# A graph-network kernel: VectorE is made to follow GpSimd's gathers, and the first gathers are issued without a copy of their indices

## The chip, the core and the metric

The kernel runs on one core of a Trainium2 chip. The metric is the device time of one execution in microseconds (us), as the median of several runs. The core has five engines with queues of their own: PE (TensorE, matmuls), DVE (VectorE), ACT (ScalarE), POOL (GpSimd) and SP (SyncE, which here only issues DMAs). They wait for each other through semaphores. A gather by a list of row indices is issued by POOL, with one instruction for each tile of 128 rows.

## What is computed

Two layers of a graph network over 3125 nodes and 53125 edges, the edges sorted by destination. Cut to what matters here, with `x` of 3125 x 256:

```python
# layer 0
messages = edge_val[:, None] * x[src]
neighbor = segment_sum(messages, dst, 3125)
side = (neighbor + neighbor * x) @ W2.T + b2
out = leaky(x @ W1.T + b1 + side)
x = layernorm(x + out / norm(out))
# layer 1
e = relu(edge_attr @ ee_w1 + ee_b1) @ ee_w2 + ee_b2
agg = segment_sum(x[src] + e, dst, 3125)
h = mlp((1 + eps) * x + agg)          # 256 -> 1024 -> 1024 -> 256, two layernorms
x = layernorm(x + relu(layernorm(x + h)))
```

## The kernel before

**Stages.** The first stage does layer 0 and the part of layer 1 that doesn't need its result (the sum over edges of `relu(edge_attr @ ee_w1 + ee_b1)`). The second stage gathers rows of the table that the first one stored, sums them and runs the three dense layers. The change touches the first stage alone.

**Tiles.** Nodes lie in 25 blocks of 128, edges in tiles of 128: 17 tiles for each block and 8 for the last, 416 in all. The tiles of a block are handled as pairs (`PAIRS`, line 41): eight pairs of two and a ninth (k = 8) of one.

**One pair (q, k) of the first stage.**
- POOL gathers the rows `x[src]` of each of its tiles into `raw[:, j]` (line 777; line 757 in the first block). Before each even j it waits for `message` of the same pair one block earlier, which freed that part of `raw`.
- ACT (`highs`, line 1408) scales each gathered tile into the high half of `msg` (line 1414), then takes relu of the edge network's result out of PSUM (line 1417).
- DVE makes the low halves: `low_neighbour` (line 1800) reads `raw` and `msg`, both in SBUF, once for each tile; `low_edge` (line 1806) reads PSUM and `msg` and counts up `message`.
- DVE also writes the one-hot matrices `oh` that say which row of the block each edge goes to (`near_oh`, line 1781, through `equal`, line 134: one tensor_scalar of 128x128 for each tile).
- PE multiplies `oh` by `msg` and adds up in PSUM (lines 932 and 934), and runs the edge network (line 927) three pairs ahead, into a ring of three banks.

**Order on DVE.** It is written out by hand in `near_block` (line 1873). In step s of block b, DVE first writes one-hots (needed three sums later), then waits for `high` of the pair three on (`LEAD = 3`) and does its `low_neighbour` and `low_edge`; pieces of the tails of the two blocks before (`tail`, line 1819: normalisation, table rows) are put in between, and `take_s` after step 1.

**Start.** SP issues `dst` (line 515), then `src` (line 516), then the rest. POOL writes two iotas (`lane`, `base`), a memset of one row of ones in `attr` (line 739, 1x2176), waits for `src`, copies the first block's indices into three small tiles (line 746) and gathers from these. DVE meanwhile checks in how many blocks the sorted edges stray (lines 1727 to 1752), which yields `level`; every engine waits for that and then takes the path for sorted edges ("near").

**End of the stage.** After its last gather POOL prepares one-hots of source rows (line 859), and then issues eight early gathers of the second stage (line 869), once the table rows of all blocks but the last two are stored; these rows come from DVE's `tail` of block 22 (line 1858), which stands behind the last messages in DVE's order.

Of the kernel before, what the change touches and what calls it, by code (L numbers as in the profile page):

```python
# [31 lines left out]
N, E, D, ED, H = 3125, 53125, 256, 64, 1024  # L32
P = 128
BLOCKS = -(-N // P)
TILES = E // N
LAST_ROWS = N - (BLOCKS - 1) * P
LAST_TILES = -(-E // P) - (BLOCKS - 1) * TILES
# [3 lines left out]
PAIRS = [(0, 2), (2, 2), (4, 2), (6, 2), (8, 2), (10, 2), (12, 2), (14, 2), (16, 1)]  # L41
NP = len(PAIRS)
# [2 lines left out]
ZERO_ROW = ROWS_PADDED  # L45
assert LAST_TILES % 2 == 0
LEAD = 3
ENDING = 3
CHUNKS = [(0, 6), (6, 6), (12, 5)]
KD = D // 128  # L50
# [7 lines left out]
def wait(eng, sem, value):  # L58

    if isinstance(value, int) and value <= 0:  # L60
        return
    eng.wait_ge(sem, value)
# [80 lines left out]
def has_pair(b, k):  # L143

    return exists(b) and (k < LAST_PAIRS or not is_last(b))
# [44 lines left out]
def gnn_program(nc, x, xT, src, dst, weight, attrT, w1T, w2T, bias01, bias02, eps_in, ee_w1, ee_b1row, ee_b1,  # L190
# [6 lines left out]
    with ExitStack() as keep:  # L197
# [14 lines left out]
        src_all = sb("src_all", [P, BLOCKS * TILES], I32)  # L212
# [16 lines left out]
        with ExitStack() as ca:  # L229
# [3 lines left out]
            def ma(name):  # L233
                return sem(name)
# [8 lines left out]
            attr = sa("attr", [ED + 1, TILES * P], F32)  # L243
            raw_base = nc.sbuf_base
            raw = sa("raw", [P, TILES, D], F32)
# [52 lines left out]
            src_in, weight_in, we1_in = ma("src_in"), ma("weight_in"), ma("we1_in")  # L298
            idx_ready = [ma(f"idx_ready{c}") for c in range(3)]
            attr_in = [ma(f"attr_in{c}") for c in range(3)]  # L300
            gathered = [ma(f"gathered{j}") for j in range(TILES)]
            xs_in, xr_in, xT_in = ma("xs_in"), ma("xr_in"), ma("xT_in")

            pool_ready = ma("pool_ready")
            prep = ma("prep")
            bad_ready, bad_total, level_ready = ma("bad_ready"), ma("bad_total"), ma("level_ready")
            rel_ready = ma("rel_ready")
# [3 lines left out]
            message = ma("message")  # L311
# [9 lines left out]
            da = ma("da")  # L321
            dd_end = [ma(f"dd_end{n}") for n in range(ENDING)]
            da_end = [ma(f"da_end{n}") for n in range(ENDING)]
# [184 lines left out]
        def _(sp):  # L508
            def load_attr(n, c):
# [2 lines left out]
                sp.dma_start(attr[0:ED, j * P:(j + m) * P],  # L512
                             attrT[:, bass.ds((n * TILES + j) * P, m * P)]).then_inc(attr_in[c], 16)

            sp.dma_start(dst_i[:, :, :].rearrange("p b j -> p (b j)"), dst).then_inc(edges_in, 16)
            sp.dma_start(src_all[:, :], src).then_inc(src_in, 16)
            sp.dma_start(w_sb[:, :], weight).then_inc(weight_in, 16)
            sp.dma_start(we1[0:ED, :], ee_w1).then_inc(we1_in, 16)
            sp.dma_start(we1[ED:ED + 1, :], ee_b1row).then_inc(we1_in, 16)
# [141 lines left out]
            with sp.If(lvl > 0):  # L661
# [11 lines left out]
                for b in range(1, BLOCKS - 1):  # L673
# [9 lines left out]
                    if 3 <= b < 3 + len(weights):  # L683
                        load, k = weights[b - 3]
# [47 lines left out]
        def _(pool):  # L732
# [2 lines left out]

            pool.iota(base[:, :], [[P, BLOCKS], [0, TILES]], base=0, channel_multiplier=0,
                      allow_small_or_imprecise_dtypes=True).then_inc(pool_ready, 1)
            pool.wait_ge(pool_ready, 2)
            pool.memset(attr[ED:ED + 1, :], 1.0).then_inc(pool_ready, 1)
            pool.wait_ge(pool_ready, 3)  # L740
            pool.wait_ge(src_in, 16)

            def stage_idx(n, c):

                j0, m = CHUNKS[c]
                pool.tensor_copy(idx[c][:, :], src_all[:, tile_cols(n, j0, m)]).then_inc(idx_ready[c], 1)

            def gather_chunk(q, c, start=0):
                j0, m = CHUNKS[c]
                pool.wait_ge(idx_ready[c], q + 1 + (1 if start else 0))  # L750
                pool.nop(nofuse=True)
                for j in range(j0, j0 + m):
                    if j % 2 == 0:

                        wait(pool, message, start + NP * (q - 1) + j // 2 + 1)
                        pool.nop(nofuse=True)
                    pool.indirect_dma_start(
                        out=raw[:, j, :], out_offset=None, in_=x,
                        in_offset=bass.IndirectOffsetOnAxis(ap=idx[c][:, j - j0:j - j0 + 1], axis=0),
                    ).then_inc(gathered[j], 16)  # L760


            for c in range(3):
                stage_idx(0, c)
            for c in range(3):
                gather_chunk(0, c)
            pool.wait_ge(level_ready, 1)
            lvl = pool.value_load(level[0:1, 0:1])

            def near_gathers(q):  # L770

                for j in range(LAST_TILES if is_last(q) else TILES):
                    if j % 2 == 0:

                        pool.wait_ge(message, NP * (q - 1) + j // 2 + 1)
                        pool.nop(nofuse=True)
                    pool.indirect_dma_start(  # L777
                        out=raw[:, j, :], out_offset=None, in_=x,
                        in_offset=bass.IndirectOffsetOnAxis(
                            ap=src_all[:, q * TILES + j:q * TILES + j + 1], axis=0),  # L780
                    ).then_inc(gathered[j], 16)

            def near_program(path):
# [4 lines left out]
            def general_program():  # L788
                for j in range(TILES):
                    pool.wait_ge(gathered[j], 16)  # L790

                def general_block(b):
                    with pool.Fori(0, BLOCKS) as n:
                        q = b * BLOCKS + n
                        for c in range(3):

                            pool.wait_ge(message, NP * q + 3 * c + 3)
                            stage_idx(n, c)
                            gather_chunk(q, c, NP)

                general_block(0)
                with pool.Fori(1, BLOCKS) as b:
                    general_block(b)
                second_general()
# [105 lines left out]
        @block.tensor  # L910
        def _(pe):

            pe.wait_ge(pool_ready, 3)
            pe.wait_ge(bad_ready, 1)
            pe.matmul(ps_d[0:1, 0:len(EDGES)], ones_c[:, :], bad_sum[:, :], start=True, stop=True)\
              .then_inc(bad_total, 1)
# [76 lines left out]
            def near_block(path, b, bank):  # L993

                for s in range(NP):
                    q, k = (b, s + LEAD) if s + LEAD < NP else (b + 1, s + LEAD - NP)
                    if has_pair(q, k):
# [13 lines left out]
            def near_program(path):  # L1011
                for k in range(LEAD):
                    edge_layer(0, k)
# [3 lines left out]
                near_block(path, before, 1)  # L1017
                edge_layer(last, LEAD)
                near_step(path, last, 0, 0)
# [376 lines left out]
        def _(act):  # L1396
# [50 lines left out]
            def near_block(path, b, par):  # L1447
                for s in range(NP):
                    q, k = (b, s + LEAD) if s + LEAD < NP else (b + 1, s + LEAD - NP)
                    if has_pair(q, k) and not (is_last(q) and k >= LEAD - 1):  # L1450
                        highs(path, q, q, k)
# [11 lines left out]
            def near_program(path):  # L1463
                for k in range(LEAD):
                    highs(path, 0, 0, k)
# [254 lines left out]
        @block.vector  # L1720
        def _(dve):

            dve.memset(ones_c[:, :], 1.0).then_inc(prep, 1)
            dve.memset(ln_eps[:, :], LN_EPS).then_inc(prep, 1)
            dve.memset(zero_oh[:, :], 0.0).then_inc(prep, 1)
# [24 lines left out]
            dve.tensor_scalar(holds[:, :], ps_d[0:1, 0:len(EDGES)], 0.0, None, ALU.is_equal).then_inc(prep, 1)  # L1750
            dve.wait_ge(prep, n_prep + 1)
            dve.tensor_tensor(level[:, :], holds[:, 0:1], holds[:, 1:2], ALU.add).then_inc(level_ready, 1)
            dve.wait_ge(pool_ready, 3)
            dve.wait_ge(level_ready, 1)
            dve.wait_ge(weight_in, 16)
            lvl = dve.value_load(level[0:1, 0:1])
# [62 lines left out]
            def tail(b, n, par, lag=1):  # L1819
# [40 lines left out]
                else:  # L1860
# [9 lines left out]
            TAIL_2 = {(1, 1): 2, (1, 2): 3, (2, 0): 4, (3, 1): 5, (3, 2): 6, (4, 1): 7, (4, 2): 8, (4, 3): 9,  # L1870
                      (6, 0): 10, (7, 1): 11}

            def near_block(path, b, bank, places=range(NP)):
                def fill(s, place):
                    if exists(b - 1) and (s, place) in TAIL_1:
                        tail(b - 1, TAIL_1[s, place], 1 - bank)
                    if exists(b - 2) and (s, place) in TAIL_2:
                        tail(b - 2, TAIL_2[s, place], bank)

                for s in places:  # L1880
                    q, k = (b, s + LEAD) if s + LEAD < NP else (b + 1, s + LEAD - NP)
                    j0, m = PAIRS[k]
                    if s <= 5:
                        near_oh(path, b, s + 3)
                    if s == 5:
                        near_oh(path, b, SUMS - 1)
                    if s >= 6 and exists(b + 1):
                        if s == 6:
                            near_oh(path, b + 1, 0)
                        if s <= 7:  # L1890
                            near_oh(path, b + 1, 1, s - 6)
                        else:
                            near_oh(path, b + 1, 2)
                    if has_pair(q, k):
                        dve.wait_ge(high, NP * q + k + 1)
                        for j in range(j0, j0 + m):
                            low_neighbour(q, j)
                    fill(s, 0)
                    if has_pair(q, k):
                        low_edge(k)  # L1900
                    for place in range(1, 4):
                        fill(s, place)
                    if s == 1 and exists(b - 1):
                        take_s(b - 1, SUMS * b, 1 - bank)
# [454 lines left out]
```

## Time and profile before

| | |
|---|---|
| median of 3 runs | 1189.99 us (1189.46 to 1193.68) |
| the profiled execution | 1194.22 us |
| its span, first to last instruction | 1192.4 us |
| first stage, up to POOL's last gather of it | 552.1 us |
| busy over the span | PE 93%, PE weight load 78%, DVE 80%, ACT 53%, POOL 71% |

How to read it: "busy" counts an instruction from its start to its end, so that one that stands blocked inside its own duration counts as busy too. An idle time is put down to what ended it: a DMA that landed, an instruction of another engine, or "issue", in which the engine waited for nothing that the profile shows. In a timeline a line "x2" is two like instructions merged into one, with their common time. For POOL's gathers, the duration is the time on the engine, and the landing of the data comes later.

### The profile page before, as it was taken

The numbers are of one execution on the slowest core, as the hardware profiler recorded it, in microseconds if no ns is written. First come the engines' busy times: TensorE is split into PE (matmuls) and PEld (weight loads), VectorE is DVE, ScalarE is ACT, GpSimd is POOL, SyncE is SP. The second block draws the span as 40 slices with busy tenths as digits, with TensorE's granted clock in tenths as the row PEclk, the third lists the DMA queues.
The fourth block names the chain that finished last, engine by engine and source line by source line (L and its number), as shares of the span: only waits on it lengthen the run. The fifth ranks groups of instructions, "written<-read, shape, count | busy, mean of one in ns | idle before, by whom it ended". The sixth has DMA issues, their size and how long they took to land.

```text
span 1192.4 us, 21565 instructions
## 1 busy us (share of the span) xinstructions
PE 1110.5 (93%) x5734; PEld 931.3 (78%) x5734; DVE 949.5 (80%) x2765; ACT 633.3 (53%) x1526; POOL 843.8 (71%) x859
## 2 busy tenths in 40 slices
PE   6899899899999999898689999999999999999996
PEld 4777677777777777677478888888888888888885
DVE  6889889888988988989657777777777777777765
ACT  4566556556656665665625445534544553455453
POOL 7777777777777777778767767776777777677700
PEclk9899999998999999999799999999999999999999
DMA  7456676676666565565867777777777677777710
GB/s 198 139 159 187 170 201 194 173 209 184 179 188 182 166 175 168 161 172 155 266 179 220 216 213 200 206 211 207 207 208 213 202 206 211 209 206 202 213 64 12
DMA packets 100813, 221.45 MB, mean 186 GB/s; under 512 B 19335, under 2 KB 50945, under 8 KB 100738
## 3 DMA queue, kind: packets, MB, share of 16 engines
q0 software_dynamic: 53408, 164.16, 49.0%
q1 hardware_dynamic: 47330, 56.46, 15.5%
q8 instruction: 27, 0.44, 0.2%
q14 instruction: 48, 0.39, 0.1%
HBM read 203.71 MB, written 16.83 MB: 185 GB/s over the span
## 4 chain that ended last, share of the span: by engine, by line
PE 49%; DVE 14%; DMA 12%; POOL 11%; issue 9%; ACT 4%; POOLq 0%; DVEq 0%; ACTq 0%; SPq 0%
PE ps_z L1155 28%; DMA raw<-in_x,src_all 11%; POOL raw L777 10%; PE ps_s L1138 9%; PE ps_y L1155 6%; DVE msg L1800 5%; PE ps_tr L1222 4%; DVE msg L1806 4%; DVE oh L134 2%; ACT msg L1414 2%; ACT msg L1417 2%; DMA grow<-table_dram,early_idx 1%; POOL grow L869 1%; PE ps_z L1190 1%; PE ps_tr L1149 0%
## 5 line engine op out<-in xcount | busy, mean ns | idle before, releaser
L831 POOL DMA_INDIRECT grow<-table_dram,src_all x410 | 401.8, 980 | 162.4 <-issue 103.1
L777 POOL DMA_INDIRECT raw<-in_x,src_all x399 | 403.3, 1011 | 121.6 <-issue 107.9
L1414 ACT ACTIVATE msg<-raw,w_sb 128x256 fp32r<-128x256 f32 x416 | 198.8, 502 | 145.6 <-DMA raw<-in_x,src_all 127.9
L1155 PE MATMUL ps_z<-w_high,a 128*128 128x512 f32 x784 | 252.3, 393 | 0.5 <-DVE a L2077 0.5
L932 PE MATMUL ps_sum<-msg,oh 128*128 128x512 f32 x464 | 229.6, 495 | 16.8 <-DVE msg L1806 16.3
L927 PE MATMUL ps_e<-we,attr 65*128 65x256 f32 x832 | 226.3, 393 | 9.3 <-DVE msg L1806 7.1
L1800 DVE SCALAR_TENSOR_TENSOR msg<-raw,w_sb,msg 128x256 fp32r<-128x256 f32 x416 | 183.7, 481 | 62.8 <-ACT msg L1417 61.6
L134 DVE TENSOR_SCALAR oh<-lane,rel 128x128 fp32r<-128x128 f32 x919 | 207.6, 300 | 0.1
L927 PEld LDWEIGHTS ps_e<-we,attr 65*128 65x128 f32 x832 | 157.2, 195 | 45.9 <-issue 21.5
L934 PE MATMUL ps_sum<-msg,oh 128*128 128x512 f32 x464 | 185.3, 399 | 0.0
L1155 PEld LDWEIGHTS ps_z<-w_high,a 128*128 128x128 f32 x784 | 147.3, 188 | 30.4 <-issue 0.9
L1556 ACT ACTIVATE aF<-ps_tr,be,g 128x128 f32<-128x128 f32 x392 | 142.4, 469 | 30.6 <-PE ps_tr L1222 30.6
L1155 PE MATMUL ps_z<-w_low,a 128*128 128x512 f32 x392 | 153.0, 390 | 0.0
L1806 DVE SCALAR_TENSOR_TENSOR msg<-ps_e,msg 128x512 fp32r<-128x512 f32 (+1 forms) x220 | 144.0, 655 | 0.0
L1417 ACT ACTIVATE msg<-ps_e 128x512 fp32r<-128x512 f32 (+1 forms) x220 | 122.6, 557 | 8.2 <-PE ps_e L927 7.7
L1138 PE MATMUL ps_s<-grow,oh 128*128 128x256 f32 x910 | 122.5, 285 | 0.2 <-DMA grow<-table_dram,src_all 0.2
L932 PEld LDWEIGHTS ps_sum<-msg,oh 128*128 128x128 f32 x464 | 89.4, 193 | 42.5 <-issue 24.6
L1138 PEld LDWEIGHTS ps_s<-grow,oh 128*128 128x128 f32 x910 | 117.0, 191 | 4.2 <-issue 0.4
L2034 DVE BATCH_NORM_STATS2 bs<-ps_z 128x6 f32<-128x512 f32 x100 | 69.5, 696 | 63.1 <-PE ps_z L1155 62.9
L1562 ACT ACTIVATE fm<-fm,ln_eps 128x1 f32<-128x1 f32 x50 | 14.7, 295 | 165.6 <-DVE fm L2039 165.6
L934 PEld LDWEIGHTS ps_sum<-msg,oh 128*128 128x128 f32 x464 | 90.0, 194 | 16.2
L1155 PEld LDWEIGHTS ps_z<-w_low,a 128*128 128x128 f32 x392 | 73.8, 188 | 13.7
(147 smaller groups left out, 1442.3 us busy)
## 6 DMA issues: line engine op xcount, KB each, us to landing
attr<-in_attrT SPq DMA_DIRECT2D x50, 192.0 KB, 4.2
grow<-table_dram,src_all POOLq DMA_INDIRECT x410, 3.7
table_dram<-table SPq DMA_DIRECT2D x25, 256.0 KB
raw<-in_x,src_all POOLq DMA_INDIRECT x399, 3.2
w_raw<-in_m_w SPq DMA_DIRECT2D x12, 512.0 KB, 6.0
attr<-in_attrT SPq DMA_DIRECT2D x24, 160.0 KB, 3.3
xs<-in_x SPq DMA_DIRECT2D x25, 128.0 KB, 2.4
xTb<-in_xT SPq DMA_DIRECT2D x25, 128.0 KB, 2.7
```

The source lines that it names most:

```text
L134: ins = dve.tensor_scalar(out_[:, i, :], lanes, which[:, i:i + 1], None, ALU.is_equal)
L777: pool.indirect_dma_start(out=raw[:, j, :], out_offset=None, in_=x, in_offset=bass.IndirectOffsetOnAxis(ap=src_all[:, q * TILES + j:q * TI ...
L831: pool.indirect_dma_start(out=grow[:, j, :].bitcast(F32), out_offset=None, in_=table_dram, in_offset=bass.IndirectOffsetOnAxis(ap=src_all[ ...
L927: mm = pe.matmul(ps_e[k % 3][:, (j - j0) * D:(j - j0 + 1) * D], attr[:, j * P:(j + 1) * P], we1[:, :], start=True, stop=True)
L932: pe.matmul(ps_sum[bank][:, :], oh[:, slot, :], msg[:, j, 0, :], start=start, stop=False, skip_group_check=True)
L934: return pe.matmul(ps_sum[bank][:, :], oh[:, slot, :], msg[:, j, 1, :], start=False, stop=stop, skip_group_check=True)
L1138: mm = pe.matmul(ps_s[:, 0:D], oh[:, path.slot[c] + j - j0, :], grow[:, j, part * D:(part + 1) * D], start=c == first and j == j0 and part ...
L1155: mm = pe.matmul(acc, left[a], right[b], start=False, stop=stop and a == 1, skip_group_check=True)
L1414: act.activation(msg[:, j, 0, 0:D], raw[:, j, :], ACT.Copy, scale=w_sb[:, tile_cols(n, j)])
L1417: act.activation(msg[:, j0:j0 + m, 0, D:2 * D], ps_e[k % 3][:, 0:m * D].rearrange("p (j d) -> p j d", d=D), ACT.Relu).then_inc(high, 1)
L1800: dve.scalar_tensor_tensor(msg[:, j, 1, 0:D], raw[:, j, :], w_sb[:, tile_cols(n, j)], msg[:, j, 0, 0:D].bitcast(F32), ALU.mult, ALU.subtract)
L1806: dve.scalar_tensor_tensor(msg[:, j0:j0 + m, 1, D:2 * D], ps_e[k % 3][:, 0:m * D].rearrange("p (j d) -> p j d", d=D), 0.0, msg[:, j0:j0 + ...
```

## The change

Three edits.

1. Each gather of the first stage also counts up a new semaphore, `issued`, when the instruction on POOL has ended (`engine_sem=issued`; `gathered` still counts the landing). In `near_block`, DVE waits, before the one-hots of a step, until the gather four tiles beyond the pair of that step has ended (`follow`, `AHEAD = 4`). Where that would be past the last tile, no wait is issued.
2. The first block's gathers take their indices directly from `src_all`; the three copies are gone from the path for sorted edges. SP issues `src` ahead of `dst`.
3. The row of ones in `attr` is written by DVE as its first instruction, no longer by POOL, with a semaphore of its own (`ones_row`) that PE waits for.

```diff
+AHEAD = 4
@@ sync
+            sp.dma_start(src_all[:, :], src).then_inc(src_in, 16)
             sp.dma_start(dst_i[:, :, :].rearrange("p b j -> p (b j)"), dst).then_inc(edges_in, 16)
-            sp.dma_start(src_all[:, :], src).then_inc(src_in, 16)
@@ gpsimd
-            pool.wait_ge(pool_ready, 2)
-            pool.memset(attr[ED:ED + 1, :], 1.0).then_inc(pool_ready, 1)
-            pool.wait_ge(pool_ready, 3)
             pool.wait_ge(src_in, 16)
...
-            for c in range(3):
-                stage_idx(0, c)
-            for c in range(3):
-                gather_chunk(0, c)
+            for j in range(TILES):
+                pool.indirect_dma_start(
+                    out=raw[:, j, :], out_offset=None, in_=x,
+                    in_offset=bass.IndirectOffsetOnAxis(ap=src_all[:, j:j + 1], axis=0),
+                    engine_sem=issued,
+                ).then_inc(gathered[j], 16)
...
                             ap=src_all[:, q * TILES + j:q * TILES + j + 1], axis=0),
+                        engine_sem=issued,
                     ).then_inc(gathered[j], 16)
@@ tensor
-            pe.wait_ge(pool_ready, 3)
+            pe.wait_ge(ones_row, 1)
@@ vector
+            dve.memset(attr[ED:ED + 1, :], 1.0).then_inc(ones_row, 1)
...
-            dve.wait_ge(pool_ready, 3)
...
+            def follow(q, k):
+
+                tiles = TILES * q + PAIRS[k][0] + PAIRS[k][1] + AHEAD
+                if not isinstance(q, int) or tiles <= TILES * (BLOCKS - 1) + LAST_TILES:
+                    dve.wait_ge(issued, tiles)
+
             def near_block(path, b, bank, places=range(NP)):
...
                     j0, m = PAIRS[k]
+                    if has_pair(q, k):
+                        follow(q, k)
                     if s <= 5:
                         near_oh(path, b, s + 3)
```

## Rows read from the trace of the kernel before

**Rows 1.** The page, costliest groups: busy, mean ns | idle before, releaser.
```profile
L777 POOL DMA_INDIRECT raw<-in_x,src_all x399 | 403.3, 1011 | 121.6 <-issue 107.9
L1414 ACT ACTIVATE msg<-raw,w_sb 128x256 fp32r<-128x256 f32 x416 | 198.8, 502 | 145.6 <-DMA raw<-in_x,src_all 127.9
```
**Rows 2.** Line 777 alone, whole span: duration ns min/median/max, then issue to landing.
```profile
L777 POOL DMA_INDIRECT raw<-in_x,src_all x399: 942/948/1874, 27.6 to 551.2; - x200
...
DMA to landing us min/median/max: 2.7/3.2/6.6
```
**Rows 3.** Waits, 100 to 500 us: us in total, times, longest.
```profile
POOL raw L777 <- issue: 80.4, 264, 0.3
...
POOL raw L777 <- DVE msg L1806: 12.2, 40, 0.3
```
**Rows 4.** Windows: PE, PEld, DVE, ACT, POOL busy, clock, DMA share, GB/s.
```profile
350.00:400.00 50.00, 47.21 (x210) 37.40 (x209) 45.59 (x134) 31.42 (x77) 38.24 (x39) 1.00 0.65 183
```
**Rows 5.** Timeline of POOL: the start, and the last gather.
```profile
2.16 1.90 POOL L739 MEMSET attr<- 1x2176 f32 x1
4.13 0.86 POOL L746 COPY idx<-src_all 128x6 int32<-128x6 int32 x3
5.26 1.18 POOL L757 DMA_INDIRECT raw<-in_x,idx  x1 [0.27 <-issue]
6.74 1.27 POOL L757 DMA_INDIRECT raw<-in_x,idx  x1 [0.30 <-issue]
...
551.16 0.95 POOL L777 DMA_INDIRECT raw<-in_x,src_all  x1 [0.30 <-issue]
```
**Rows 6.** Timeline, DVE and POOL, around 118 us: a lengthened gather.
```profile
118.21 0.45 DVE L134 TENSOR_SCALAR oh<-lane,rel 128x128 fp32r<-128x128 f32 x2
118.58 0.87 DVE L1800 SCALAR_TENSOR_TENSOR msg<-raw,w_sb,msg 128x256 fp32r<-128x256 f32 x2
...
118.66 1.21 POOL L777 DMA_INDIRECT raw<-in_x,src_all  x1 [0.30 <-issue]
```
**Rows 7.** The same, around 176 us: one-hots that begin as a gather ends.
```profile
175.60 0.48 DVE L134 TENSOR_SCALAR oh<-lane,rel 128x128 fp32r<-128x128 f32 x2
175.99 0.88 DVE L1800 SCALAR_TENSOR_TENSOR msg<-raw,w_sb,msg 128x256 fp32r<-128x256 f32 x2
...
174.55 1.02 POOL L777 DMA_INDIRECT raw<-in_x,src_all  x1 [0.30 <-issue]
175.88 1.02 POOL L777 DMA_INDIRECT raw<-in_x,src_all  x1 [0.30 <-issue]
177.20 0.94 POOL L777 DMA_INDIRECT raw<-in_x,src_all  x1 [0.30 <-issue]
```
**Rows 8.** The same, around 262 us: the longest kind of gather.
```profile
262.17 0.48 DVE L134 TENSOR_SCALAR oh<-lane,rel 128x128 fp32r<-128x128 f32 x2
262.56 0.88 DVE L1800 SCALAR_TENSOR_TENSOR msg<-raw,w_sb,msg 128x256 fp32r<-128x256 f32 x2
...
262.38 1.87 POOL L777 DMA_INDIRECT raw<-in_x,src_all  x1 [0.31 <-issue]
```
**Rows 9.** Timeline, end of the first stage: POOL, then DVE.
```profile
548.44 1.16 POOL L777 DMA_INDIRECT raw<-in_x,src_all  x1 [0.30 <-issue]
...
547.57 0.69 DVE L134 TENSOR_SCALAR oh<-lane,rel 128x128 fp32r<-128x128 f32 x3
...
550.03 0.47 DVE L134 TENSOR_SCALAR oh<-lane,rel 128x128 fp32r<-128x128 f32 x2
...
558.67 0.88 DVE L1800 SCALAR_TENSOR_TENSOR msg<-raw,w_sb,msg 128x256 fp32r<-128x256 f32 x2 [0.15 <-ACT msg L1417]
```
**Rows 10.** The chain that ended last, 540 to 610 us: start, us, what.
```profile
560.15 0.34 DVE table L1858
...
560.55 2.04 DMA table_dram<-table
...
563.40 1.05 POOL grow L869
...
572.54 7.30 DMA grow<-table_dram,early_idx
```
**Rows 11.** Timeline of DVE and SP, the start.
```profile
0.74 0.40 SPq L515 DMA_DIRECT2D dst_i<-in_dst  x1
...
0.89 0.17 DVE L1725 MEMSET zero_oh<- 128x128 f32 x1
3.23 1.07 DVE L1727 CAST dst_f<-dst_i 128x425 f32<-128x425 int32 x1 [2.18 <-DMA dst_i<-in_dst]
...
10.04 0.48 DVE L1907 MEMSET s_r<- 128x512 f32 x1 [0.91 <-DVE level L1752]
```

More of the change, by code:

```diff
@@ L301, in gnn_program @@
             gathered = [ma(f"gathered{j}") for j in range(TILES)]
+            issued = ma("issued")
             xs_in, xr_in, xT_in = ma("xs_in"), ma("xr_in"), ma("xT_in")
             pool_ready = ma("pool_ready")
+            ones_row = ma("ones_row")
             prep = ma("prep")
@@ L746, in stage_idx, with gather_chunk @@
                 pool.tensor_copy(idx[c][:, :], src_all[:, tile_cols(n, j0, m)]).then_inc(idx_ready[c], 1)
-            def gather_chunk(q, c, start=0):
+            def gather_chunk(q, c):
                 j0, m = CHUNKS[c]
-                pool.wait_ge(idx_ready[c], q + 1 + (1 if start else 0))
+                pool.wait_ge(idx_ready[c], q + 1)
                 pool.nop(nofuse=True)
@@ L753, in gather_chunk @@
                     if j % 2 == 0:
-                        wait(pool, message, start + NP * (q - 1) + j // 2 + 1)
+                        pool.wait_ge(message, NP * q + j // 2 + 1)
                         pool.nop(nofuse=True)
@@ L798, in general_block @@
                             stage_idx(n, c)
-                            gather_chunk(q, c, NP)
+                            gather_chunk(q, c)
                 general_block(0)
```

## The prediction

> **What bounds the kernel now.** I read the costliest groups first, then the waits and the timeline of the first stage, and last the chain that ended last. PE is busy 93% of the span, but busy time doesn't show what sets the pace of the first stage. ACT stands idle 127.9 us before line 1414 because a gather hasn't landed [rows 1]. The gathers come from POOL, and POOL never waits for anybody: between 100 and 500 us every idle time before line 777 is 0.3 us at most, also where DVE is named as releaser [rows 3]. From its first gather at 5.26 us to the end of the last at 552.11 us POOL issues 416 gathers with only that gap between them [rows 5]. So the first stage lasts as long as POOL's queue: 416 x (duration + 0.30 us). The duration has a floor: minimum 942 ns, median 948 ns; the mean is 1011 ns [rows 1, 2]. The 63 ns between mean and median, times 399, are 25.1 us, and this is the only time that the order of DVE's work can win from POOL.
>
> **What lengthens a gather.** I laid each of the 416 gathers beside DVE's instructions. A gather at 118.66 took 1.21 us while a `low_neighbour` (two inputs in SBUF) that began 0.08 us before it was under way [rows 6]. Its counterparts that begin 0.35 to 0.1 us ahead of a gather lengthen it by 0.04 to 0.26 us, those that begin 0.35 to 0.6 us into it by nothing; `low_edge`, which reads PSUM, at the gather's start lengthens nothing. So the phase of DVE against POOL matters, and edit 1 sets the phase.
>
> **Edit 1: does the wait bind?** I took, for each step with such a wait, the time at which DVE began its one-hots and the end of the gather that it must now see. In 164 of 215 steps DVE began earlier, by 1.6 us on average and 3.2 at most. The last two are 547.57 against a gather that ended at 549.60, and 550.03 against 552.11 [rows 9]. So the wait binds in some three of four steps. What is queued behind it on DVE: one-hots, `low_neighbour`, `low_edge`, the tail pieces and `take_s`. Who waits for these: PE's sums and its edge network, ACT's `norm`, `deviation` and `table_high`, SP's stores, and POOL through `message`. POOL asks for the message of the same pair one block back, some seven pairs, or 18 us, behind where a bound DVE stands: a delay of 3.2 us doesn't reach it. DVE doesn't fall behind for good either: it is busy 45.59 of 50 us in the fullest window [rows 4], and the start-to-start times of its instructions add up to 19.8 us for a block that takes POOL 17 x 1.315 = 22.4 us. Only after step 4, which holds 2.8 us of work ahead of a step that is due one gather later, it is late by 1.5 us, and catches up in the next. So the wait costs POOL nothing by itself, and the DVE work keeps pace.
>
> **What the phase is worth.** A bound step begins its one-hots just after a gather has ended. The nearest rows are those where this happened anyway: the one-hots at 175.60 follow a gather that ended at 175.57; the next gather took 1.02 us, the one after it 0.94 [rows 7]. There are 38 such places (one-hots 0.20 to 0.29 us ahead of a gather). In 35 of them the two gathers are together 0.09 us over 0.95; in three the first took 1.87 us [rows 8], and with these the average is 0.16. All gathers of the stage together are 0.126 us over for every two. The saving is then 0.126 - 0.088 = 0.038 us for every two gathers, 208 x 0.76 x 0.038 = 6.0 us. I take this value because the three long ones stood behind an uninterrupted row of DVE work, where a bound step has an idle DVE ahead of it. Bounds: all of the excess gone, 25.1 us; or 0.16 in place of 0.126, which costs 208 x 0.034 = 7.1 us. The semaphore that each gather now counts up on POOL isn't shown by any row. From below: it is free, as the gap of 0.30 us may hold it; from above, one DVE instruction's wait for its neighbour, about 0.03 us, on 416 gathers, 12.5 us. I take 0, since the gap is the same 0.3 whether a wait for DVE stands in it or not [rows 3], so it has room for more than issuing.
>
> The Trainium skill bears on this (page "SBUF — State Buffer", section "Who interferes with whom"): a DVE tensor_scalar in a two-port mode and any GpSimd instruction lock each other out, while a DVE instruction with two SBUF inputs disturbs only GpSimd instructions that read SBUF; the page infers that writing descriptors isn't disturbed by them. By that, only the one-hots would hurt, and moving them into the 0.30 us gap would win the whole excess. The rows speak against it in part: the lengthened gathers go with `low_neighbour` [rows 6]. It is rival A.
>
> **Edits 2 and 3: the start.** Gone from POOL ahead of the first gather are the memset (1.90 us) and the copies (0.86 us) [rows 5]. What is late next is `src`: the first load was issued at 0.74 us, and the work that waited for it began at 3.23 [rows 11]; `src` now has that place, so the first gather begins at about 3.4 in place of 5.26: 1.9 us. More of the gathers now lie beside DVE's checks; the first two, which did already, took 1.18 and 1.27 us [rows 5], so I take off 0.1 and keep 1.8 us; 1.3 if all five that now lie there are like that. `dst` comes 0.45 us later and `level` with it; POOL needs it only after 17 gathers. The memset on DVE: 128 elements took 0.17 us and 512 took 0.48 [rows 11], so 2176 take about 1.8 us, from 0.8 to 2.7, ahead of the arrival of `dst` at about 3.7; without this cover it would cost its 1.8 us on `level`, and even then nothing on POOL.
>
> **The end of the stage.** Here the wait costs. After the last gather the chain runs through DVE: the last messages, the table rows at 560.15, their store, and only then POOL's early gathers at 563.40 [rows 10]. Between the last two waits and the table rows DVE has hardly a gap; the only idle ahead of line 1800 is 0.15 us [rows 9]. DVE now begins these two steps 2.0 and 2.1 us later as seen from POOL's last gather. Of that 0.1 is covered: +2.0 us. It falls due once. What comes after (early gathers, second stage, where no instruction is changed) shifts as a whole.
>
> **The sum**, against the profiled execution of 1194.2 us: -6.0 (phase), -1.8 (start), +2.0 (end) = -5.8, so 1188.4. The profiled execution lies 4.2 us above the median of the runs; against the median it is 1190.0 - 5.8 = 1184.2 us.
>
> **Rivals.** **A, the whole excess goes:** -25.1 - 1.8 + 2.0 = -24.9, 1165 us; half of it, 1177. For it speaks that a bound DVE is idle in the gather's last part; against it that `low_neighbour` still follows the one-hots by 0.39 us, into the next gather's start, and that 0.07 was lost in just that place [rows 7]. **B, the phase is a bad one:** if the one-hots begin 0.08 us after the gather's end in place of 0.03, `low_neighbour` lies as in rows 8. Of 21 such places three lost 0.92 us, and the average of the two gathers was 0.21 over: 208 x (0.21 - 0.126) = +17.5 us, 1207 us. It decides from the point at which a pair of gathers costs over 0.126. The phase in a bound step hangs on how fast a semaphore of POOL reaches DVE, which no row shows. **C, nothing comes of it:** DVE's tail pieces shift the steps after the wait so that phases are as mixed as before; start and end cancel: 1190 us. It also covers a wait that is passed before it binds. **D, the semaphore lengthens each gap on POOL:** 0.03 x 416 = 12.5 us more than the forecast, 1197 us.
>
> **How the numbers follow.** Chances: forecast 0.42, A in whole or half 0.17, B 0.11, C 0.20, D 0.10. What is within 0.5% (6 us, about what a measurement of this kernel can tell from no change) is 1184 to 1196. The forecast lies at that edge: half of its chance counts as faster, half as the same. With A and a little of C: faster 0.42. With C and some of D: same 0.40; slower 0.18. The range leaves out the full A and the full B: 1172 to 1199.
>
> **What would show it.** Right: mean of line 777 near 0.99 us with gaps of 0.30, first gather near 3.4 us, one-hots 0.03 to 0.1 us behind a gather's end in most steps, more DVE idle put down to line 777, and POOL's early gathers 13 us behind its last gather of the stage in place of 11.3. Wrong: a gap above 0.30, a mean above 1011 ns, more gathers over 1.8 us, POOL waiting for line 1806, or a second stage of another length.

## The result and the profile after

The changed kernel takes 1177.74 us (median of 4 runs, 1176.62 to 1179.83) against 1189.72 us (1188.5 to 1193.68) of the kernel before on the same chip: ratio 0.9896, 95% interval 0.9869 to 0.9923, some 12 us or 1.0% less. The forecast was 1184.2 us in a range of 1172 to 1199: the time lies in it, on the side forecast, and the gain is twice the 5.8 us of the sum. The ratios and intervals here and below are taken over the fast executions alone of a kernel that also has a slower state, and so needn't be the quotient of the medians beside them. Between the two profiled executions the spans differ by 14.4 us (1192.4 to 1178.0); the one of before lay 4.2 us above its median, that of after 2.1.

The costliest groups of the page after (busy, mean ns | idle before, releaser), to be read beside [rows 1]:

```profile
L778 POOL DMA_INDIRECT raw<-in_x,src_all x399 | 389.5, 976 | 121.6 <-issue 108.5
...
L135 DVE TENSOR_SCALAR oh<-lane,rel 128x128 fp32r<-128x128 f32 x919 | 212.0, 301 | 24.3 <-DMA raw<-in_x,src_all 24.0
L1416 ACT ACTIVATE msg<-raw,w_sb 128x256 fp32r<-128x256 f32 x416 | 194.4, 501 | 69.7 <-DMA raw<-in_x,src_all 60.4
L1802 DVE SCALAR_TENSOR_TENSOR msg<-raw,w_sb,msg 128x256 fp32r<-128x256 f32 x416 | 182.8, 477 | 15.9 <-ACT msg L1419 14.3
```

Three things stand in these rows. The mean gather fell from 1011 to 976 ns, and the idle time before it is 121.6 us as before: the semaphore on POOL costs nothing. The one-hots, which never waited, now wait 24 us; the profile puts this down to the gather's DMA, but it is the new wait for the end of the instruction on POOL. ACT's idle ahead of line 1416 halved, but none of it was saved: up to 560 us ACT is idle 219 us in place of 222, and what is gone ahead of this line now stands ahead of others of ACT's lines, which wait for the later DVE. The long gathers are gone: the longest takes 1.29 us, against 1.87 in [rows 2].

Line 778 alone over the whole span (duration ns min/median/max):

```profile
L778 POOL DMA_INDIRECT raw<-in_x,src_all x399: 942/946/1292, 25.3 to 535.0; - x200
```

The start, the last gather and the first early gather in POOL's timeline, beside [rows 5] and [rows 10]:

```profile
1.25 0.84 POOL L739 IOTA base<- 128x425 f32 x1
3.63 1.10 POOL L763 DMA_INDIRECT raw<-in_x,src_all  x1 [1.53 <-DMA src_all<-in_src]
5.04 0.95 POOL L763 DMA_INDIRECT raw<-in_x,src_all  x1 [0.31 <-issue]
...
535.03 1.03 POOL L778 DMA_INDIRECT raw<-in_x,src_all  x1 [0.30 <-issue]
...
549.48 1.05 POOL L871 DMA_INDIRECT grow<-table_dram,early_idx  x1 [3.08 <-DMA table_dram<-table]
```

This splits the 14.4 us of the two spans. The first gather begins at 3.63 in place of 5.26: -1.6. From there to the end of the last gather it is 532.4 us in place of 546.9: -14.4. From the last gather to the first early gather 13.4 us in place of 11.3: +2.1. The rest of the span is 628.5 in place of 629.0: -0.5.

**A bound step**, that is one in which DVE comes to the new wait before the gather has ended and is held. Timeline of POOL after, around 302 us:

```profile
301.47 0.95 POOL L778 DMA_INDIRECT raw<-in_x,src_all  x1 [0.30 <-issue]
302.72 0.95 POOL L778 DMA_INDIRECT raw<-in_x,src_all  x1 [0.30 <-issue]
303.97 0.95 POOL L778 DMA_INDIRECT raw<-in_x,src_all  x1 [0.30 <-issue]
```

and of DVE in the same stretch:

```profile
302.45 0.53 DVE L135 TENSOR_SCALAR oh<-lane,rel 128x128 fp32r<-128x128 f32 x2 [0.25 <-DMA raw<-in_x,src_all]
302.90 0.87 DVE L1802 SCALAR_TENSOR_TENSOR msg<-raw,w_sb,msg 128x256 fp32r<-128x256 f32 x2
303.69 0.68 DVE L1808 SCALAR_TENSOR_TENSOR msg<-ps_e,msg 128x512 fp32r<-128x512 f32 x1
```

The one-hots begin 0.03 us after the gather's end at 302.42, and `low_neighbour` 0.18 us into the next gather. I laid all steps beside the gathers as for the prediction: in 110 of 207 the one-hots begin within 0.12 us of the end of the gather that they wait for, and there both gathers that follow take 0.947 us on average: none is lengthened. (Of each of the two one-hots the line shows only the common time: the first begins at 302.45, 0.27 us ahead of the next gather, the second 0.07 us ahead of it.) In the other 97 steps the two together are 0.12 us over 0.95, as all steps were before. 110 x 0.13 us is the 14 us. What all gathers take over 0.95 us, those below it counted as nothing, is 12.2 us (26.1 before); this is called the excess from here on.

**Where it remains.** Steps 5 and 6 of a block (the ninth pair and the one after it) begin about 1.7 and 0.2 us late, behind step 4 with its 2.8 us of work, and step 2, behind `take_s`, 0.34 us late; these three are late in nearly every block, steps 3, 4 and 7 in about half of them. POOL and DVE there:

```profile
293.59 1.18 POOL L778 DMA_INDIRECT raw<-in_x,src_all  x1 [0.30 <-issue]
295.07 1.03 POOL L778 DMA_INDIRECT raw<-in_x,src_all  x1 [0.30 <-issue]
296.40 1.01 POOL L778 DMA_INDIRECT raw<-in_x,src_all  x1 [0.30 <-issue]
```

```profile
293.52 0.43 DVE L1857 TENSOR_TENSOR tb<-x,eb 128x256 f32<-128x256 f32 x1
293.86 0.48 DVE L135 TENSOR_SCALAR oh<-lane,rel 128x128 fp32r<-128x128 f32 x2
...
295.71 0.88 DVE L1802 SCALAR_TENSOR_TENSOR msg<-raw,w_sb,msg 128x256 fp32r<-128x256 f32 x2
296.51 0.42 DVE L1860 TENSOR_TENSOR table<-tb,table 128x256 fp32r<-128x256 f32 x1
```

At the start of the gather of 1.18 us a tail piece with two inputs in SBUF is under way (line 1857, begun 0.07 us before it), like `low_neighbour` in [rows 6]. Put down to the DVE instruction that was begun last before the gather, `low_neighbour` has 6.5 us of what is left, the tail pieces 4.5 and the one-hots 1.1.

### The profile page after: what moved, and what is told of

Read it like the earlier page. It is cut to its first block, busy times and chain, and to the rows that moved or that the text cites. A ratio compares the mean times of both kernels' runs of the same rounds, so it can differ in the third digit from the quotient of the medians.

```text
span 1178.0 us, 21743 instructions
## 1 busy us (share of the span) xinstructions
PE 1109.2 (94%) x5734; PEld 925.7 (79%) x5734; DVE 960.2 (82%) x2766; ACT 627.8 (53%) x1526; POOL 826.8 (70%) x855
## 4 chain that ended last, share of the span: by engine, by line
PE 53%; DVE 15%; POOL 10%; issue 9%; DMA 9%; ACT 3%; SPq 1%; DVEq 0%; POOLq 0%; ACTq 0%
PE ps_z L1157 29%; POOL raw L778 10%; PE ps_s L1140 9%; DMA raw<-in_x,src_all 7%; PE ps_y L1157 6%; DVE msg L1802 5%; PE ps_tr L1224 4%; DVE msg L1808 4%; DVE oh L135 2%; PE ps_e L929 2%; ACT msg L1416 1%; ACT msg L1419 1%; PE ps_sum L934 1%; PE ps_sum L936 1%; DVE x L1854 1%
## 5 line engine op out<-in xcount | busy, mean ns | idle before, releaser
L778 POOL DMA_INDIRECT raw<-in_x,src_all x399 | 389.5, 976 | 121.6 <-issue 108.5
L135 DVE TENSOR_SCALAR oh<-lane,rel 128x128 fp32r<-128x128 f32 x919 | 212.0, 301 | 24.3 <-DMA raw<-in_x,src_all 24.0
L1416 ACT ACTIVATE msg<-raw,w_sb 128x256 fp32r<-128x256 f32 x416 | 194.4, 501 | 69.7 <-DMA raw<-in_x,src_all 60.4
L929 PEld LDWEIGHTS ps_e<-we,attr 65*128 65x128 f32 x832 | 154.4, 194 | 51.7 <-issue 27.5
L1419 ACT ACTIVATE msg<-ps_e 128x512 fp32r<-128x512 f32 (+1 forms) x220 | 122.6, 557 | 12.0 <-PE ps_e L929 11.8
L1564 ACT ACTIVATE fm<-fm,ln_eps 128x1 f32<-128x1 f32 x50 | 14.8, 295 | 166.6 <-DVE fm L2049 166.6
```

Of the source, the lines that this page charges most:

```text
L135: ins = dve.tensor_scalar(out_[:, i, :], lanes, which[:, i:i + 1], None, ALU.is_equal)
L778: pool.indirect_dma_start(out=raw[:, j, :], out_offset=None, in_=x, in_offset=bass.IndirectOffsetOnAxis(ap=src_all[:, q * TILES + j:q * TI ...
L929: mm = pe.matmul(ps_e[k % 3][:, (j - j0) * D:(j - j0 + 1) * D], attr[:, j * P:(j + 1) * P], we1[:, :], start=True, stop=True)
L1416: act.activation(msg[:, j, 0, 0:D], raw[:, j, :], ACT.Copy, scale=w_sb[:, tile_cols(n, j)])
```

## The experiments

The theory under test: what lengthens a gather is a DVE instruction with two SBUF inputs at a certain phase of the gather, and the wait helps because it fixes that phase (**phase**). Rivals: the one-hots, a tensor_scalar, block POOL and are moved into POOL's gap (**one-hots**); DVE being later helps, whatever the phase (**delay**); the start gives more than it shows.

Runs that stand in one table shared a chip and the runs of the kernel before.

**1. No wait.** The changed kernel without edit 1's wait:

```diff
-                    if has_pair(q, k):
-                        follow(q, k)
```

> The changed kernel without DVE's wait (follow is not called); the semaphore on the gathers, the direct indices, the load order and the moved memset stay. Both theories of edit 1 expect the mean of the gathers to come back to about 1.01 us (excess over 0.95 about 25 us) and a total of 1.6 us (start) below the kernel before, some 1188 us, the end of the stage giving back nothing as DVE isn't held. If the start had a larger share in the gain than the 1.6 us that the first gather shows (3.63 against 5.26), the time would be well below 1188.

**2. The wait alone.** The kernel before, with the semaphore on its gathers and `follow` as in the change, and nothing of edits 2 and 3.

> The kernel before with edit 1 alone (semaphore and wait; POOL's memset, the index copies and the load order as before). If the wait makes the gain: mean of the gathers about 0.977 us, about 1.6 us above the changed kernel, some 1179.5 us. If the edits need each other: near 1188.

**3. The wait behind the one-hots.**

```diff
-                    if has_pair(q, k):
-                        follow(q, k)
                     if s <= 5:
                         near_oh(path, b, s + 3)
...
                     if has_pair(q, k):
+                        follow(q, k)
                         dve.wait_ge(high, NP * q + k + 1)
```

> The changed kernel with the wait moved behind the one-hots of the step, ahead of the wait for ACT. The one-hots then lie anywhere, and low_neighbour begins about 0.03 us after a gather's end, 0.27 before the next, where it lengthened that by 0.07 to 0.13 us in the kernel before. Theory 'phase of low_neighbour' (two SBUF inputs): excess of the two gathers of a bound step about 0.1 us, total 1184 to 1192. Theory 'one-hots out of the way' (tensor_scalar blocks POOL, low_neighbour doesn't): the one-hots are no longer in the gap and the excess is back as well, but the lengthened gathers are those with one-hots under way, not those with low_neighbour at their start. A third, 'any alignment does': time as the changed kernel, 1178.

**4. The last block free.**

```diff
-                    if has_pair(q, k):
+                    if has_pair(q, k) and not is_last(q):
                         follow(q, k)
```

> The changed kernel without the wait for the pairs of the last block. If holding DVE at the end costs what the traces show (13.4 us from the last gather to the first early gather against 11.3), this gives back up to 2.1 us: first early gather 11.3 to 11.8 us behind, total 1175.7 to 1176.5. If something else sets that distance: no change, 1178.

Measured (kernel before: 1191.44 us):

| | us | ratio, 95% interval | mean gather, ns | excess, us | last gather to first early gather, us |
|---|---|---|---|---|---|
| 1 no wait | 1189.56 | 0.9990 (0.9976 to 1.0004) | 1005 | 23.4 | 11.3 |
| 2 wait alone | 1179.00 | 0.9897 (0.9871 to 0.9924) | 971 | 10.6 | 13.4 |
| 3 wait behind the one-hots | 1188.34 | 0.9980 (0.9963 to 0.9997) | 999 | 21.0 | 13.2 |
| 4 last block free | 1176.46 | 0.9882 (0.9853 to 0.9911) | 971 | 10.2 | 13.4 |

Runs 1 and 2 come out as the theory has it: the wait alone makes the gain (1.0%), and the start brings 1.9 us of median, which this measurement can't tell from nothing. Run 3 holds `low_neighbour` at the same gathers, yet nearly all of the gain is gone; so it isn't the delay, nor any alignment. In 102 of its 207 steps `low_neighbour` begins 0.03 us behind a gather's end, and there the next gather is 0.083 us over 0.95 and the one after it 0. One of them, POOL and DVE of run 3:

```profile
299.61 1.09 POOL L778 DMA_INDIRECT raw<-in_x,src_all  x1 [0.30 <-issue]
301.00 1.02 POOL L778 DMA_INDIRECT raw<-in_x,src_all  x1 [0.30 <-DVE msg L1808]
302.33 0.94 POOL L778 DMA_INDIRECT raw<-in_x,src_all  x1 [0.30 <-issue]
303.57 1.03 POOL L778 DMA_INDIRECT raw<-in_x,src_all  x1 [0.30 <-issue]
```

```profile
300.74 0.47 DVE L135 TENSOR_SCALAR oh<-lane,rel 128x128 fp32r<-128x128 f32 x2
301.12 0.88 DVE L1802 SCALAR_TENSOR_TENSOR msg<-raw,w_sb,msg 128x256 fp32r<-128x256 f32 x2
...
303.31 0.87 DVE L1802 SCALAR_TENSOR_TENSOR msg<-raw,w_sb,msg 128x256 fp32r<-128x256 f32 x2
```

`low_neighbour` at 303.31 begins 0.26 us ahead of the gather of 1.03 us; at 301.12 it begins 0.12 us into a gather, and that took 1.02 us, as in [rows 7]. In the bound step of the changed kernel it is 0.18 us into the gather, and that costs nothing. What does the harm at 301.00 is not `low_neighbour`, though, but the one-hot that is under way there: see run 5.

Run 4 missed its expectation in the distance, which stayed at 13.4 us. Its two waits don't hold DVE: the last `low_neighbour` of the last of these steps begins 0.8 us behind the last gather's end with them and without. The waits up to there have already made DVE late, and the steps that follow hold as much work as POOL's last gathers leave time. Its time lies in the range expected, but for another reason: not at the end, but in its gathers, of which 133 steps are like the bound one above, in place of 110 in the changed kernel, with the same waits. The 1.3 us between the medians of two sets of runs can't be told from nothing.

**5. The second SBUF input taken away**, on the kernel before, without any wait for gathers:

```diff
-                dve.scalar_tensor_tensor(msg[:, j, 1, 0:D], raw[:, j, :], w_sb[:, tile_cols(n, j)],
+                dve.scalar_tensor_tensor(msg[:, j, 1, 0:D], ps_e[j // 2 % 3][:, 0:D], w_sb[:, tile_cols(n, j)],
```

> The kernel before (no wait, old start), with low_neighbour reading its first input from PSUM (a bank of the edge network) in place of raw; the low halves of the messages are then not what they should be, everything else is computed as before. One-hots, tail pieces and all waits stay. If it is the second SBUF input of low_neighbour that lengthens gathers: the excess over 0.95 us, 26 us in the kernel before, falls to the share of the tail pieces with two SBUF inputs, 2 to 8 us, the mean to 0.955 to 0.97 us, and the total to 1167 to 1173 us, with no wait for the gathers at all. If the one-hots (tensor_scalar) do it: excess and time stay, 1190.

> The same kernel as e5_psum_input, since on the chip of that run the kernel before itself took 1575 us and POOL didn't set the pace, so that its total says nothing. The low halves of the messages are again not what they should be. Expected where the kernel before takes about 1190 us: mean of the gathers 0.955 to 0.965 us (its excess of 26 us down to some 4.5, as on that chip), total 1167 to 1172 us if low_neighbour's second SBUF input is what lengthens gathers; 1190 if the one-hots do.

**6. AHEAD = 5.**

> The changed kernel with AHEAD = 5: each step one gather later. Theory 'phase': phases as with 4, ACT is always ready, mean 0.970 to 0.977 us; the end of the stage 1.25 us longer (first early gather 14.7 us behind the last gather): 1177.5 to 1179.5 us. Theory 'the delay helps': mean below 0.965, total below 1176. If DVE's slack doesn't do for it, POOL shows waits for messages and the time is above 1185.

> As e9_ahead5, where POOL sets the pace: phases as with 4, mean of the gathers 0.970 to 0.977 us, first early gather 14.7 us behind the last gather of the stage, 1177.5 to 1179.5 us. If it is the delay that helps and not the phase: mean below 0.965, below 1176 us.

Measured on the chip on which the kernel before takes 1189.55 us:

| | us | ratio, 95% interval | mean gather, ns | excess, us | last gather to first early gather, us |
|---|---|---|---|---|---|
| 5 input from PSUM | 1173.15 | 0.9862 (0.9841 to 0.9883) | 962 | 6.7 | 11.8 |
| 6 AHEAD = 5 | 1176.18 | 0.9892 (0.9871 to 0.9913) | 965 | 7.7 | 14.8 |

Run 5 computes the low halves from the wrong input, with as many instructions as before; `low_neighbour` takes 478 ns (481 before). Line 777 of this run:

```profile
L777 POOL DMA_INDIRECT raw<-in_x,src_all x399: 942/946/1202, 27.1 to 531.2; - x200
```

The excess falls from 26.1 to 6.7 us, so that most of it was the second SBUF input of `low_neighbour`. The total is 1 us above what was expected. But the one-hots aren't innocent, as the rest of this run shows. A gather with one-hots at its start and no instruction with two SBUF inputs near it:

```profile
264.24 0.68 DVE L1806 SCALAR_TENSOR_TENSOR msg<-ps_e,msg 128x512 fp32r<-128x512 f32 x1
264.84 0.47 DVE L134 TENSOR_SCALAR oh<-lane,rel 128x128 fp32r<-128x128 f32 x2
264.92 1.02 POOL L777 DMA_INDIRECT raw<-in_x,src_all  x1 [0.30 <-issue]
265.23 0.87 DVE L1800 SCALAR_TENSOR_TENSOR msg<-ps_e,w_sb,msg 128x256 fp32r<-128x256 f32 x2
```

In this run 56 gathers are lengthened by 0.02 to 0.12 us with a one-hot as the last instruction begun before them, 3.3 us in all, nearly all where that one-hot began 0.07 to 0.13 us ahead; the tail pieces with two SBUF inputs make 3.1 us. In the kernel before, `low_neighbour` has 17.8 us in 116 gathers and the one-hots 5.9 us in 40, of which the three long gathers are 2.8. So both the phase theory and rival A's reading hold in part: the larger part is `low_neighbour`, the smaller the one-hots.

Run 6 keeps the phase and moves every bound step by one gather. Its one-hots begin 0.03 us behind a gather's end in 134 of 211 steps, more than the 110 of the changed kernel; but runs 2 and 4 have 127 and 133 with AHEAD = 4, so that this isn't the doing of AHEAD alone. The tail piece `tb` of step 4 still meets a gather's start, in 21 gathers with 3.0 us in all; what is smaller is `low_neighbour`'s part, 2.7 us in place of 6.5. A bound step costs as little as with 4. Here from its timelines of POOL and DVE:

```profile
299.83 0.94 POOL L778 DMA_INDIRECT raw<-in_x,src_all  x1 [0.30 <-issue]
301.08 0.95 POOL L778 DMA_INDIRECT raw<-in_x,src_all  x1 [0.30 <-issue]
302.33 0.95 POOL L778 DMA_INDIRECT raw<-in_x,src_all  x1 [0.30 <-issue]
```

```profile
300.81 0.53 DVE L135 TENSOR_SCALAR oh<-lane,rel 128x128 fp32r<-128x128 f32 x2 [0.25 <-DMA raw<-in_x,src_all]
301.26 0.87 DVE L1802 SCALAR_TENSOR_TENSOR msg<-raw,w_sb,msg 128x256 fp32r<-128x256 f32 x2
```

The time was expected at 1177.5 to 1179.5 and is 1176.2, since the mean came out at 965 ns, below the expected 970. That is at the edge of what **delay** was to give (below 965 ns and 1176 us), so the total doesn't decide between the two; the bound steps and run 3 do. The end is 1.35 us longer, for a wait 1.25 us later. Against the changed kernel (ratios 0.9892 and 0.9896) no difference can be told.

**7. Runs on two chips on which another thing sets the pace.** Five kernels ran, one of them twice, where the kernel before itself takes 1575 and 1577 us. Three of these were not run elsewhere:

> The changed kernel with AHEAD = 3: DVE may start each step one gather (1.25 us) earlier. Theory 'phase': a bound step still begins 0.03 us behind a gather's end, so its two gathers cost 0; but more steps then find ACT not ready and low_neighbour begins at any time: bound and clean steps 60 to 100 in place of 110, mean 0.98 to 0.995 us, end of the stage up to 1.2 us shorter: 1179 to 1185 us. Theory 'it is the delay that helps, not the phase': excess in proportion to the delay, half way back, 1184 and above, also in bound steps.

> The same kernel as e6_two_free (AHEAD = 4, no wait for the pairs of the last two blocks), where POOL sets the pace. If the wait's hold on DVE makes the longer end: first early gather 11.3 to 12.2 us behind the last gather of the stage in place of 13.4, mean of the gathers 0.972 to 0.977, total 1175 to 1176.5 us. If the distance stays at 13.4 us, something else makes it, and the total stays at 1177 to 1178.

> Three edits on the changed kernel: AHEAD = 5; no wait for the pairs of the last two blocks; the one-hot of the last sum step written in step 2, which has slack, in place of step 5, which is short. With 5 the gathers left over 0.95 us are the ones beside steps 6 and 7, which start 0.3 us late behind steps 4 and 5; 0.2 us less work in step 5 should bring step 6 to within 0.1 us of a gather's end. Phase theory: mean 0.955 to 0.966 us, first early gather 11.3 to 12.8 us behind the last, total 1172.5 to 1175.5 us. If the shift of step 6 puts its low_neighbour or the table row into a worse place: mean 0.967 to 0.975, 1175.5 to 1178.

The kernel with the last two blocks free ran twice; this was expected of it the first time:

> The changed kernel without the wait for the pairs of the last two blocks. Freeing the last block alone left the distance at 13.4 us, since DVE had been held up to the step before and has no gap there in which to gain it back. Freed one block earlier, DVE can gain its 1.5 us of idle per block: distance 11.3 to 12.2 us; one more block of mixed phases costs about 0.6 us. Total 1.0 to 1.5 us below that of freeing one block. If the distance stays at 13.4, it isn't the wait that makes it.

| | us | kernel before, us | ratio, 95% interval |
|---|---|---|---|
| AHEAD = 3 | 1575.77 | 1575.20 | 1.0007 (0.9967 to 1.0046) |
| AHEAD = 5 | 1574.28 | 1575.20 | 0.9988 (0.9949 to 1.0027) |
| last two blocks free | 1573.27 | 1575.20 | 1.0005 (0.9970 to 1.0039) |
| last two blocks free, again | 1574.21 | 1577.36 | 0.9970 (0.9940 to 1.0000) |
| AHEAD = 5, last two blocks free, one-hot moved | 1580.98 | 1577.36 | 0.9999 (0.9947 to 1.0050) |
| input from PSUM | 1586.83 | 1575.20 | 1.0112 (1.0052 to 1.0173) |

There POOL isn't the bound any more. Waits of the run with AHEAD = 5, from 100 to 500 us (us in total, times, longest):

```profile
ACT msg L1419 <- remote: 98.2, 21, 10.0
POOL raw L778 <- DVE msg L1808: 91.7, 37, 6.6
DVE msg L1802 <- ACT msg L1419: 72.7, 15, 7.3
POOL raw L778 <- issue: 65.8, 205, 1.6
DVE msg L1802 <- issue: 47.2, 17, 7.8
```

"Remote" is a releaser that stands in no record of the core. ACT and DVE stand for 5 to 10 us at a time for it or for nothing that the profile shows, the others follow, and POOL waits for messages, which it never did in [rows 3]. In at most one of some 215 steps of a run does DVE reach the new wait before it is fulfilled, and so neither the wait nor its variants change the time. What the price of one gather is can be read even there: the excess is 4.5 us with the input from PSUM and 26.0 with AHEAD = 3. What stops the engines on these chips isn't known from these runs, nor why the input from PSUM is 1.1% slower there. AHEAD = 3, the last two blocks free and the combination in the last row but one (the one meant to beat both kernels) have no verdict where POOL sets the pace.

## Why the prediction was right, and where it was off

**What bounds the first stage:** right. Without a wait of POOL anywhere, 416 gathers of (duration + 0.30 us) are the stage: the 14.4 us that it lost are the fall of the mean (34 ns x 416 = 14 us).

**The phase term was mis-sized:** 6.0 us forecast, 14.4 in the trace. The step that failed is the price of a bound step. I took it from 38 places where one-hots happened to begin as a gather ended (0.088 us for the two gathers), and took these for the same thing. They aren't. In the twelve places like [rows 7] the second one-hot began 0.08 us ahead of the gather and `low_neighbour` 0.11 to 0.12 us into it, as DVE came out of other work; that cost 0.07. It is the one-hot's doing, since run 5 has the same cost in the same place with `low_neighbour` reading PSUM. A bound step starts from idle: its second one-hot begins 0.067 us ahead, takes 0.05 us longer, `low_neighbour` follows at 0.18, and the cost is 0.00. Some 0.01 us of phase decide. The rows had both prices for `low_neighbour` at 0.17 to 0.19 (up to 0.175 us: seven times 0.12 us and three times 0.92; from 0.180 on: seven times nothing), which should have widened the term rather than been averaged. In the other direction, fewer steps are bound than the three in four of the prediction (110 of 207): steps 2, 5 and 6 arrive late; the prediction had it for step 5 alone.

So the mechanism came as forecast, with the harmless phase set by the wait, but its size didn't: that the time lies in the range is owed to its width, which takes in half of rival A.

**The start:** forecast -1.8, trace -1.6; the first gather came at 3.63, not 3.4. `level` didn't come later: see the last section.

**The end:** forecast +2.0, trace +2.1, and its size follows the wait (no wait 11.3 us, AHEAD = 4 13.4, AHEAD = 5 14.8). The prediction blamed the last two waits; run 4 shows that these two alone don't make it. That freeing more blocks would give it back wasn't shown.

**The semaphore:** forecast 0, and the gap is 0.30 us with and without it.

**The rivals.** A (the one-hots, from the rule of the Trainium skill, page "SBUF — State Buffer", section "Who interferes with whom", and its inference that writing descriptors isn't disturbed by a second SBUF input): run 5 speaks against the inference for these gathers, since the second SBUF input of `low_neighbour` carries some three quarters of the excess. The rule on tensor_scalar agrees in part: the one-hots lengthen gathers as well, by 3.3 us in run 5, but only when begun just ahead of one; that they run in a two-port mode no run here shows. Still, the size that it gave for half of the excess (1177 us) is what came. B (a bad phase) is what run 3 made by hand: 1188 us. C and D didn't occur where POOL sets the pace; C is what happened on the two slower chips.

## What to carry to other kernels

Where GpSimd's gathers set the pace, sum up what their durations exceed the median by: here this was what the order on VectorE cost, and no engine's idle time shows it. A wait for the end of a gather, put where it makes VectorE's instructions fall into a harmless phase, cost only 2 us once, at the end of the stage, as VectorE had slack. An input in PSUM won more, without a wait, in a run that read the wrong data; what it costs to bring the right data there wasn't measured. A phase taken from look-alike places must match to some 0.01 us, or be tried.

## What the hardware showed that was not expected

**What a gather loses.** Take the DVE instruction that was begun last before a gather. If it is a one-hot, a `low_neighbour` from SBUF or a tail piece with two full SBUF inputs (`tb`, `y`, `table`), still under way, and begun more than 0.07 us ahead, the gather takes longer by the time from its own start to the start of DVE's next instruction, less 0.043 us. With anything else it takes its 0.946 us. This gives 96% of the 3304 durations of the eight traces in which POOL sets the pace to within 0.012 us. An example is the gather at 118.66 in [rows 6]: the next `low_neighbour` begins 0.313 us into it, so it should lose 0.270, and takes 1.208 us, 0.262 more than 0.946. If the instruction begins later, the gather mostly loses nothing and the instruction does: the second one-hot of a bound step takes 0.326 us in place of 0.28. So it looks as if whichever comes first goes first. The rule was read out of the traces afterwards and no run was made to test it; it doesn't hold everywhere (34 of 612 one-hots begun later did cost, 0.03 to 0.93 us, among them the long gathers like [rows 8]), and why these do stays open.

**A bound step lies at the edge.** Its second one-hot begins 0.067 us ahead of the gather in the median; a one-hot begun 0.074 to 0.09 us ahead cost 0.07 us nearly everywhere in these traces. A phase earlier by 0.01 us might have made the change worth less.

**The other direction of the same contention.** DVE's conversion of `dst` took 1.07 us in [rows 11], while POOL ran its memset and copies. With these gone it takes 0.38 (0.38 in run 1 too, which has the same start; 0.92 in run 2, which has the old one), which pays for the later load, so that `level` comes at the same time (DVE's timeline after):

```profile
1.25 1.87 DVE L1725 MEMSET attr<- 1x2176 f32 x1 [1.25 <-PEq L2361]
...
3.89 0.38 DVE L1730 CAST dst_f<-dst_i 128x425 f32<-128x425 int32 x1 [0.50 <-DMA dst_i<-in_dst]
...
8.99 0.15 DVE L1755 TENSOR_TENSOR level<-holds 1x1 int32<-1x1 f32 x1
```

**Chips differ.** In three sets of runs the kernel before takes 1189.5 to 1191.4 us, on two other chips 1575 and 1577, with stops of 5 to 10 us that nothing in the program releases.
